# Attention on one core: softmax sums folded in groups of four pairs, the high half rounded on ScalarE, and the loads of queries, keys and values spread over the tiles

## The reference, cut to what matters

```python
def _L1_cond_ref(hidden, w, ln_g, ln_b, Wg, bg, Wb, bb, Wqkv, bqkv, Wp, bp, W1, b1, W2, b2, num_heads):
    ...
    h = _sln(hidden, w, ln_g, ln_b, Wg, bg, Wb, bb)
    qkv = (h @ Wqkv.T + bqkv).reshape(B, N, num_heads, hd, 3)
    ...
    energy = jnp.einsum('bhqd,bhkd->bhqk', q, k)
    att = jax.nn.softmax(energy, axis=-1) / D ** 0.5
    out = jnp.einsum('bhqk,bhkd->bhqd', att, v)
    out = jnp.moveaxis(out, 1, 2).reshape(B, N, D)
    out = out @ Wp.T + bp
```

## Time and profile before

| | us |
|---|---|
| median of three runs (2966.49 to 2967.79) | 2967.44 |
| the profiled execution's own time | 2969.34 |
| its span, first to last instruction | 2967.5 |
| TensorE busy | 2871.1 |
| VectorE, GpSimd, ScalarE busy | 2006.8, 1800.6, 1508.7 |
| mean granted TensorE clock, share of full | 0.987 |

### The profile page before, as it was taken

How to read it: one execution, slowest core, us unless ns; L and a number is a source line. 1 busy time by engine, 2 the same in 40 slices (tenths; PEclk the granted TensorE clock), 3 DMA queues, 4 the chain that set the end, 5 groups by cost and what they waited for, 6 DMA issues and landing times.

```text
span 2967.5 us, 41315 instructions
## 1 busy us (share of the span) xinstructions
PE 2871.1 (97%) x15018; PEld 1921.9 (65%) x15018; DVE 2006.8 (68%) x3559; ACT 1508.7 (51%) x2756; POOL 1800.6 (61%) x797
## 2 busy tenths in 40 slices
PE   4899999999999999999999999999999999999997
PEld 2787788888888887855555555555555555555456
DVE  6873332232233555778888888888888888888648
ACT  3552233232333322146666666666666666666654
POOL 2676310111110333148999999898989898898954
PEclk8899999999999999999999999999999999999999
DMA  6443100000001567476668866587866788666668
GB/s 218 173 142 128 43 27 2 29 29 29 29 16 56 192 217 226 163 188 124 136 136 189 174 150 144 123 185 164 182 126 142 152 186 177 138 134 138 164 199 296
DMA packets 155050, 405.64 MB, mean 137 GB/s; under 512 B 12101, under 2 KB 30505, under 8 KB 134342
## 3 DMA queue, kind: packets, MB, share of 16 engines
q0 software_dynamic: 22608, 164.64, 28.1%
q1 hardware_dynamic: 132248, 238.41, 25.8%
HBM read 144.51 MB, written 92.31 MB: 80 GB/s over the span
## 4 chain that ended last, share of the span: by engine, by line
PE 54%; DVE 2%; ACT 0%; DMA 0%; issue 0%; DVEq 0%; SPq 0%; ACTq 0%
PE psum L1727 18%; PE psum L1739 16%; PE psum L1712 16%; PE psum L1767 3%; PE psum L37 1%; PE psum L39 1%; PE psum L38 1%; DVE part_max L1848 0%; DVE p_h L2154 0%; DMA p_att_lo<-att_parts 0%; ACT probs L1818 0%; DVE p_stats L2160 0%; DVE p_h L2148 0%; DVE p_var L2171 0%; PE psum L1718 0%
## 5 line engine op out<-in xcount | busy, mean ns | idle before, releaser
L1848 DVE TENSOR_REDUCE part_max<-psum 128x1 f32<-128x512 f32 x1984 | 1212.5, 679 | 165.2 <-PE psum L1712 159.8
L1818 ACT ACTIVATE probs<-psum 128x512 f32<-128x512 f32 x2048 | 1042.4, 614 | 477.7 <-PE psum L1727 476.3
L1962 POOL TENSOR_TENSOR pair<-probs 128x2048 f32<-128x2048 f32 x204 | 937.0, 4593 | 143.2 <-ACT probs L1818 138.1
L1727 PE MATMUL psum<-queries,keys 128*128 128x512 f32 x2048 | 838.9, 412 | 8.8 <-PEq L2358 3.1
L1712 PE MATMUL psum<-keys,queries 128*128 128x512 f32 x1984 | 788.9, 398 | 0.9 <-DVE part_max L1848 0.3
L1727 PEld LDWEIGHTS psum<-queries,keys 128*128 128x128 f32 x2048 | 382.8, 187 | 341.0 <-issue 214.3
L1739 PE MATMUL psum<-probs,values 128*32 128x512 f32 x4096 | 510.7, 599 | 0.0
L1081 DVE TENSOR_TENSOR h_lo<-w_stage,h_hi 128x512 fp32r<-128x512 f32 x128 | 101.8, 796 | 485.4 <-ACT h_hi L989 485.3
L1712 PEld LDWEIGHTS psum<-keys,queries 128*128 128x128 f32 x1984 | 373.6, 188 | 78.8 <-DVE part_max L1848 20.4
L982 ACT ACTIVATE w_stage<-psum,b_col 128x512 f32<-128x512 f32 x128 | 88.3, 690 | 483.8 <-PE psum L39 482.9
L1739 PEld LDWEIGHTS psum<-probs,values 128*32 128x32 f32 x4096 | 106.9, 109 | 240.8 <-issue 122.1
(11 more groups left out here) (342 smaller groups left out, 3836.7 us busy)
## 6 DMA issues: line engine op xcount, KB each, us to landing
pair<-pair POOLq DMA_DIRECT2D x94, 1024.0 KB, 8.2
raw_weight<-pair POOLq DMA_DIRECT2D x32, 1024.0 KB, 8.2
pair<-raw_weight POOLq DMA_DIRECT2D x31, 1024.0 KB, 8.2
queries<-q_parts SPq DMA_DIRECT2D x96, 256.0 KB, 9.6
keys<-k_parts SPq DMA_DIRECT2D x42, 512.0 KB, 13.1
s_x<-in_x_dram SPq DMA_DIRECT2D x8, 1024.0 KB, 7.6
s_y<-in_x_dram SPq DMA_DIRECT2D x8, 1024.0 KB, 6.1
y_rows<-s_y SPq DMA_DIRECT2D x8, 1024.0 KB, 4.7
```

The source lines that it names most:

```text
L1727: nc.tensor.matmul(psum[:, SC + unit % 3, :], keys[place(count)[0]][:, h, kt * P:(kt + 1) * P], queries[count % NQ][:, h, :], start=True, ...
L1818: act.activation(probs[tile % NPROB][:, h, :], psum[:, SC + unit % 3, :], ACT.Exp).then_inc(exp_ready, 1)
L1848: dve.tensor_reduce(part_max[:, h * TT + qt, kc:kc + 1], max_slot(), AX.X, ALU.max).then_inc(max_read, 1)
L1962: pool.tensor_tensor(pair[number % NPAIR][:, :, :], probs[2 * number % NPROB][:, :, :], probs[(2 * number + 1) % NPROB][:, :, :], ALU.add) ...
```

## The change

1. **Groups of four.** All blocks but the last fold pairs (0, 1, 2, 3) and (4, 5, 6, 7). `LAST_LAG` goes and `SUM_LAG` is 8 for all: totals stand on tile 15 and on tile 7 of the next block. GpSimd adds the fourth pair of a group in two halves, with the fold of the third pair between them; the fold onto the fourth pair is issued after the first pair add of the next group.
2. **Rounding.** The high part `att_hi` is made by ScalarE on tile 3 after head 1 (for the last two blocks at the end), not by GpSimd; GpSimd waits for it. The denominators are turned on tile 9 and inverted and spread on tile 11, where it was 11 and 13.
3. **Loads.** In block n SyncE issues the three rows of queries for block n+2 behind tiles 1, 4 and 7, the second half of keys in the block after an `ends` block behind tiles 2, 5 and 8, the values two blocks after it behind tile 3, the store of block n-2 behind tile 9, and the first half of keys in an `ends` block behind tiles 10, 11 and 14. `scored(count, n)` waits until n tiles of the block have their scores.

```diff
-    AV_LAG, SUM_LAG, LAST_LAG = 3, 10, 8
+    AV_LAG, SUM_LAG = 3, 8
...
-              for group in (((0, 1, 2), (3, 4, 5), (6, 7)) if count < BLOCKS - 1 else ((0, 1), (2, 3), (4, 5), (6, 7)))]
+              for group in (((0, 1, 2, 3), (4, 5, 6, 7)) if count < BLOCKS - 1 else ((0, 1), (2, 3), (4, 5), (6, 7)))]
...
         for count in range(BLOCKS):
...
+            renewed = count + NQ - 1
+            for row in range(3):
+                scored(count, 1 + 3 * row)
+                if count > 0 and renewed < BLOCKS:
+                    load_queries(renewed, row)
+                    if row == 2:
+                        clear_row(renewed)
+                if ends(count - 1):
+                    scored(count, 2 + 3 * row)
+                    load_keys(group(count - 1) + 1, place(count - 1)[0], 1, row)
+                if row == 0 and ends(count - 2):
+                    scored(count, 3)
+                    sp.wait_ge(av_ready, NKT * (count - 1))
+                    load_values(group(count - 2) + 1, place(count - 2)[0])
+            if count > 1:
+                scored(count, 9)
+                store(count - 2)
+            if ends(count):
+                for n in range(2):
+                    scored(count, 10 + n)
+                    load_keys(g + 1, b, 0, n)
             if count < BLOCKS - 1:
                 load_max_row(count + 1)
+            if ends(count):
+                scored(count, 14)
+                load_keys(g + 1, b, 0, 2)
...
-            sp.wait_ge(sc_ready, UNITS * (count + 1))
-            if ends:
-                load_keys(g + 1, b, 1)
-            if count + NQ < BLOCKS:
-                load_queries(count + NQ)
-            if ends:
-                sp.wait_ge(av_ready, NKT * (count + 1))
-                load_values(g + 1, b)
-            if count > 0:
-                store(count - 1)
...
+        def split_high(count):
+
+            act.wait_ge(weighed, count + 1)
+            act.wait_ge(att_st, 32 * (count + 1))
+            act.activation(att_hi[:, :], att[:, :], ACT.Copy).then_inc(att_split, 1)
...
+                if count > 1 and kt == 3 and h == 1:
+                    split_high(count - 2)
...
+            if count > 0 and kt == 9:
+                turn_sums(count - 1)
             if count > 0 and kt == 11:
-                turn_sums(count - 1)
-            if count > 0 and kt == 13:
                 invert(count - 1)
                 spread_inverse(count - 1)
...
         def split_result(count):
-            pool.wait_ge(weighed, count + 1)
-            pool.wait_ge(att_st, 32 * (count + 1))
-            pool.tensor_copy(att_hi[:, :], att[:, :]).then_inc(att_split, 1)
             pool.wait_ge(att_split, count + 1)
...
+            nth = GROUPS[OF[number]].index(number)
+            if nth == 3:
+                pool.tensor_tensor(target[:, 0:HG // 2, :], even[:, 0:HG // 2, :], odd[:, 0:HG // 2, :], ALU.add).then_inc(half_made, 1)
+                fold(number - 1)
+                pool.wait_ge(half_made, OF[number] + 1)
+                pool.tensor_tensor(target[:, HG // 2:HG, :], even[:, HG // 2:HG, :], odd[:, HG // 2:HG, :], ALU.add).then_inc(pair_ready, 1)
+            else:
+                pool.tensor_tensor(target[:, :, :], even[:, :, :], odd[:, :, :], ALU.add).then_inc(pair_ready, 1)
+            if nth == 1 and number in FOLDS:
                 fold(number)
-            if number - 1 in FOLDS and number - 2 in FOLDS:
+            if nth == 0 and number > 0 and len(GROUPS[OF[number - 1]]) == 4:
                 fold(number - 1)
```

More of the change, by code:

```diff
@@ L1562, in attention_stage @@
     inverted, spread = sem("den_inverted"), sem("inverse_spread")
-    weighed, att_split = sem("att_weighed"), sem("att_split")
+    weighed, att_split, half_made = sem("att_weighed"), sem("att_split"), sem("half_made")
     SC, MX, OUT = 0, 3, 7
@@ L1587, in fold_wait @@
         engine.wait_ge(folded[n % 2], 16 * (n // 2 + 1))
-    SUMMED_AT = {2 * group[-1] + 1 + (SUM_LAG if group[-1] < PAIRS * (BLOCKS - 1) else LAST_LAG): g for g, group in enumerate(GROUPS[:DIRECT])}
+    SUMMED_AT = {2 * group[-1] + 1 + SUM_LAG: g for g, group in enumerate(GROUPS[:DIRECT])}
     WP_AT = (BLOCKS - 1) * NKT + 3
@@ L1603, in sync, with load_keys @@
     def sync(sp):
-        def load_keys(g, b, half):
+        def load_keys(g, b, half, n):
             src = k_dram.rearrange("e (g h d) t -> e g d h t", h=HG, d=HD)
             at, n_tok = half * (L // 2), L // 2
-            for n, part in enumerate((0, 1, 0)):
-                sp.dma_start(keys[b][n * HD:(n + 1) * HD, :, at:at + n_tok].bitcast(F32),
-                             src[part, g, :, :, b * L + at:b * L + at + n_tok]).then_inc(k_ld[b][half], 16)
+            sp.dma_start(keys[b][n * HD:(n + 1) * HD, :, at:at + n_tok].bitcast(F32),
+                         src[n % 2, g, :, :, b * L + at:b * L + at + n_tok]).then_inc(k_ld[b][half], 16)
         def load_values(g, b):
@@ L1613, in load_values, with load_queries @@
                          v_dram[b * L:(b + 1) * L, g * P:(g + 1) * P].rearrange("(n p) c -> p n c", p=P)).then_inc(v_ld[b], 16)
-        def load_queries(count):
+        def load_queries(count, row):
             src = q_dram.rearrange("e (g h d) t -> e g d h t", h=HG, d=HD)
@@ L1618, in load_queries, with clear_row @@
             at = b * L + chunk * CH
-            for row, part in enumerate((0, 0, 1)):
-                sp.dma_start(queries[count % NQ][row * HD:(row + 1) * HD, :, :].bitcast(F32),
-                             src[part, group(count), :, :, at:at + CH]).then_inc(q_ld[count % NQ], 16)
+            sp.dma_start(queries[count % NQ][row * HD:(row + 1) * HD, :, :].bitcast(F32),
+                         src[row // 2, group(count), :, :, at:at + CH]).then_inc(q_ld[count % NQ], 16)
+        def clear_row(count):
             zero, row = (queries[count % NQ][n:n + 1, :, :].bitcast(F32) for n in (R + 1, R))
@@ L1650, in sync @@
         sp.wait_ge(rows_zero, 1)
-        load_queries(2)
+        for row in range(3):
+            load_queries(2, row)
+        clear_row(2)
         for half in range(2):
-            load_keys(0, 1, half)
+            for n in range(3):
+                load_keys(0, 1, half, n)
         for stored in v_st:
@@ L1656, in sync, with ends, scored @@
         load_values(0, 1)
+        def ends(count):
+            return count >= 0 and place(count)[1] == NCH - 1 and group(count) < NG - 1
+        def scored(count, tiles):
+            sp.wait_ge(sc_ready, UNITS * count + HG * tiles)
         for count in range(BLOCKS):
-            b, chunk = place(count)
-            g = group(count)
-            ends = chunk == NCH - 1 and g < NG - 1
-            if ends:
-                sp.wait_ge(sc_ready, UNITS * count + UNITS // 2)
-                load_keys(g + 1, b, 0)
+            b, g = place(count)[0], group(count)
+            renewed = count + NQ - 1
+            for row in range(3):
+                scored(count, 1 + 3 * row)
[17 more added lines that the diff above has]
+                    load_keys(g + 1, b, 0, n)
             if count < BLOCKS - 1:
                 load_max_row(count + 1)
+            if ends(count):
+                scored(count, 14)
+                load_keys(g + 1, b, 0, 2)
             if count >= BLOCKS - B:
@@ L1677, in sync @@
                     later["load_rows"](sp, 0, 0)
-            sp.wait_ge(sc_ready, UNITS * (count + 1))
-            if ends:
-                load_keys(g + 1, b, 1)
-            if count + NQ < BLOCKS:
-                load_queries(count + NQ)
-            if ends:
-                sp.wait_ge(av_ready, NKT * (count + 1))
-                load_values(g + 1, b)
-            if count > 0:
-                store(count - 1)
+        scored(BLOCKS - 1, NKT)
+        store(BLOCKS - 2)
         later["load_rows"](sp, 0, 1)
@@ L1824, in scalar @@
                 act.activation(later["wt_hi"][:, k, :], psum[:, MX + WP_SLOTS[k] % NMX, :], ACT.Copy).then_inc(whi_ready, 1)
+        split_high(BLOCKS - 2)
         copy_out(BLOCKS - 1)
+        split_high(BLOCKS - 1)
     def vector(dve):
@@ L1953, in gpsimd @@
                 normalise(count - 1)
-            if p == 6 and count == BLOCKS - 1:
-                split_result(count - 1)
             pool.wait_ge(exp_ready, 2 * HG * (number + 1))
@@ L1961, in gpsimd @@
                 fold_wait(pool, FOLDS[old + 1])
-            pool.tensor_tensor(pair[number % NPAIR][:, :, :], probs[2 * number % NPROB][:, :, :],
-                               probs[(2 * number + 1) % NPROB][:, :, :], ALU.add).then_inc(pair_ready, 1)
-            if number in FOLDS and number - 1 not in FOLDS:
+            target, even, odd = pair[number % NPAIR], probs[2 * number % NPROB], probs[(2 * number + 1) % NPROB]
+            nth = GROUPS[OF[number]].index(number)
[7 more added lines that the diff above has]
+            if nth == 1 and number in FOLDS:
                 fold(number)
-            if number - 1 in FOLDS and number - 2 in FOLDS:
```

(2 more changed lines are left out.)

## The result

The changed kernel takes 2988.0 us (median of four, 2980.5 to 2990.1) where the kernel before takes 2967.6 beside it: 1.0062 of before, 95% interval 1.0049 to 1.0074. That is 20 us slower. The forecast was 2943.7 us, faster, in a range to 2958.

A forecast was written before the change was run, and what follows sets the result against it. TensorE's work was taken to bound each block of 48.9 us. From the median of 2967.44 us, -26.7 for totals and +3 for values gave 2943.7 us, in a range of 2939.5 to 2958.

The forecast's parts named there:

- Totals removed: On TensorE in blocks 0 to 30, two groups for three: 31 totals of 0.86 us go, -26.7 us.
- Keys come in rows of 512 KB beside first folds: First folds have 9.8 us and 3.6 us of GpSimd slack behind them: cost 0, at most 6 us.
- Values beside a last fold: Values issued behind tile 3 in six blocks delay the last fold by 0.5 us each time: +3 us.
- The last block: One total leaves it, counted in the gain; its store slips about 3 us under the final normalisation, cost 0.
- Denominators earlier: The transposition of 0.70 us on tile 9 meets 0.87 us idle: cost 0, at most 0.3 a block, 9 us.
- Margins: Before totals on tiles 7 and 15 the last fold may take 9.65 us; 7.0 beside no load, at most 9.1.
- Rival 1: Moved loads stall totals in some blocks: 2961.7 us at most, typically 2953; chance 0.22 together with rival 3.
- Rival 2: TensorE waits for the last fold at tiles 7 and 15 every time: 2975 to 3006 us; chance 0.08 above 2973.
- Rival 3: GpSimd sets the pace, 0.4 us a block too long, 12 us: 2953; chance 0.22 together with rival 1.
- Rounding: ScalarE's 0.6 us on tile 3 fits its gap of 1.64 us: cost 0; without the gap 19 us.
- loads moved by themselves: Rows of queries issued one at a time have 13 us and land in under 11: cost 0.
- The estimate of 4.4 us: A 1 MB fold: 2.0 us plus its bytes at 436 GB/s; would leave over five microseconds spare and no stall.

The follow-up runs named there:

- fours_where_light: Kernel before with groups of four only in 19 blocks without keys or values, rounding on ScalarE, lag 10, loads in bursts: 2953.4 us, 0.9939 of before.
- last_total_late: Kernel of den_late with one total, that of block 30's last group, moved from tile 7 to tile 9 of the last block: 2973.4 us, 1.0015 of before.
- lag10_den_late: Changed kernel with totals ten tiles behind their group instead of eight, denominators turned on tile 11 and inverted on 13: 2962.9 us, 0.9983 of before.
- threes_lag8: Kernel before with all totals eight tiles behind their group instead of ten, groups of three, loads in bursts: 2983.4 us, 1.0039 of before.
- loads_back: Changed kernel with loads and stores in one burst at the end of a block, as in the kernel before: 3022.6 us, 1.0184 of before.
- den_late: Changed kernel with only the denominators back on tiles 11 and 13: 2980.8 us, 1.0048 of before.
- keys_second_half: Changed kernel with the three rows of the second half of keys issued behind tiles 10, 12 and 14: 2983.8 us, 1.0062 of before.

## Why the prediction was wrong

- **Totals removed, -26.7 us: right.** 31 totals of 0.86 us went, beats are 5.75; fours_where_light got 19 of them in full.
- **"Keys come in rows of 512 KB beside first folds ... 0, at most 0.5 in twelve blocks, 6 us": this step failed.** I had set the keys against GpSimd's slack of 3.6 us a block and priced one fold at a time. But each fold of the chain is asked for by GpSimd before it can issue the next, so lateness adds up: 2.8 + 2.2 us in block 24, then a third fold of 9.3. Measured: 19 us of waits in blocks 5 to 24 and 5 us by the clock; without key loads 0.8. Both parts of the lateness are in the trace. In blocks 6, 8, 16, 22 and 24 the last fold was issued so late that 5.3 to 8.5 us were left of 9.95. In blocks 5, 7 and 13 it was issued in time or nearly so and took 10.1 to 10.9 itself. The time that a first fold has was worked out as 9.8 (20.5 less 10.8 is 9.7); in block 24 it was 9.2, and the fold took 11.5. The trace of before had a warning that I did not use: a fold beside the second half of the keys and a burst of queries took 15.0, and the worst that I had priced was the 12.2 of the earlier trace rows:

```profile
L1945 POOL DMA_DIRECT2D pair<-pair x1: 870/870/870, 1591.7 to 1591.7; - x1
...
DMA to landing us min/median/max: 15.0/15.0/15.0
```

- **The worry was put on the wrong load.** Values beside a last fold, for which I took +3 us, cost at most 0.7 in the changed kernel, in block 9.
- **The last block was not in the sum.** I counted its total as one more gain, and its store as the only thing late; the 4 MB of loads for the projection, which stood in the kernel before beside folds with a longer lag, made a wait of 5.7 us and at most 3.4 us of clock. last_total_late shows 7.4 to 7.5.
- **The clock was not in the sum.** The rows of before have no half clock behind the stage's start, and a wait was priced 1:1. Waits of 2.7 us and more cost up to 1.7 times their length here (block 24: 4.1 of waiting, 7.1 over an ordinary block). Not each wait did: block 6 waited 2.7 at full clock.
- **Denominators earlier: "0, at most 0.3 a block": it was the upper bound**, 0.27. I had laid the transposition of tile 9 into its gap, and not asked what the inverse and its spreading would meet on tile 11.
- **Margins: the mechanism was right.** 9.65 us for the last fold was worked out; in the trace it is 9.95 on tile 7 and 10.6 on tile 15 of ordinary blocks, and totals waited where the last fold took over 10 us or was issued late. Rival 1 had this mechanism, at 21 us at most; it measured 25 and the clock. Rival 2, which carried the slower side, did not happen: in the blocks with queries alone no total waited. Rival 3, GpSimd's pace, is what lag10_den_late found in three blocks.
- **Rounding, and loads moved by themselves: 0, right** (0.9991 and 1.0000, both with groups of three and lag 10). GpSimd per block was forecast at 44.4 and is 44.7.
- The estimate of 4.4 us for a transfer of 1 MB (the Trainium skill, DMA: Bandwidth & Descriptors, "Anatomy of one DMA — SWDGE (gpsimd) path") is below all folds of the trace, the fastest of which took 6.9; the measurement decides.

Still open is why a fold beside keys is issued and yet lands so late, in 9 to 13 us, whether smaller rows of keys would help (no run varied their size), and what values do beside keys.

## What to carry to other kernels

When work on the bounding engine is removed by making a chain of transfers longer, sum the landings along the chain at the place where the heaviest loads stand, not the cover of each transfer in an ordinary stretch. Keep the consumer's distance when the chain grows: two tiles of lag were worth about half of what the removed totals gave (threes_lag8, 13 of 27 us). And take the gain only where the resource is free: 19 blocks of 31 gave 16 to 18 us against the kernel before beside them; all 31 gave 5 to 6 at the longer lag and lost 20 at the thin one.

## What the runs showed of the hardware

In this stage, where TensorE otherwise hardly stood, its granted clock fell to 0.5 (the lower of its two levels) at single waits: for 3.4 us at the wait of 2.7 in block 16 of the changed kernel, for 6.8 us at those of 4.1 and 5.7, and for 6.8 to 10.2 us at those of 6.0 to 7.1 in loads_back. Among the shorter waits some had it and some had not: 2.0 us in block 13 of den_late did, 2.7 in block 6 of the changed kernel and 3.0 in block 17 of keys_second_half did not.

A fold of 1 MB from one pair buffer onto another landed 7.0 us after its issue beside no load, 9.3 to 11.5 in the chain of block 24 beside single rows of keys and queries, 13.0 behind the 4 MB for the projection, and 15.0 in the burst of before.

The changed kernel scattered more than fours_where_light, 2980.5 to 2990.1 us against 2952.5 to 2954.5, four runs each. But loads_back, with the most waits, ran from 3019.5 to 3023.3, so that waits cause the scatter is not shown.
